# Half of the state's sums behind the scores in two slots of four, products in two halves by tables, and the slots' rows filled from the opening on

## The chip, the cores and the metric

The kernel runs on one core of a Trainium2 chip. The metric is the device time of one execution in microseconds (us), and the median of several executions is what is compared.

## The reference

One transformer block with adaptive layer norm, x of 4 batches by 2048 tokens by 256 features, all in float32:

```
h   = layernorm(x) * (1 + ca) + sa                 # sa, ca, ga, sb, cb, gb from silu(c) @ wmod
q,k,v = h @ w_qkv.T, 16 heads of 16;  q, k = elu(.) + 1
S_t = S_(t-1) + k_t v_t^T ;  z_t = z_(t-1) + k_t   # causal linear attention
o_t = (S_t^T q_t) / max(z_t . q_t, 1e-6)
x   = x + ga * (o @ w_out.T)
h   = layernorm(x) * (1 + cb) + sb
gates: softmax over 8 experts, top 2, capacity 1280 rows for each expert
x   = x + gb * sum over kept experts of gate * (silu(h @ w_gate.T) @ w_down[e].T)
```

## The kernel before

**Stages.** The 8192 tokens are 64 tiles of 128 tokens, and four tiles are a group (16 groups). An opening loads inputs and weights and makes the modulation rows. The attention stage then runs `slot_(it, j, n)` for n = -8 to 73, one tile to a slot (`run_slots`); q = n % 4 says which of the four slots of a group it is. A last stage runs the experts over 40 blocks of 256 gathered rows. Each engine has its own `slot_` in its own order, and the engines meet by semaphores alone.

**A slot on TensorE** (the `slot_` of `block.tensor`), for tile n, in this order: `scores(n)` (32 small products, line 1375; two heads at a time, written to the banks of `SCW`); `from_state(n)` (32 small products, line 1408: what the state from all earlier tiles gives, written to the other half of the same banks, in two rounds `other` = 0 and 1 of 16, the second behind semaphore `scores_run`; its end gives `sc_full`); `columns_and_keys(n)` (lines 1387, 1393); the first projection of the next group (`stage1_qk` m = 0 in q = 1 and m = 2 in q = 2, line 1513; `stage1_v` u = 0 in q = 3, line 1524); in q = 0 `h2_transposes` instead (line 1547), in q = 3 also `positions` (lines 1635 to 1639); `add_to_state(n)` (32 products, line 1458: the state's increment by tile n + 1); `from_tile(n)` (64 products, line 1425: masked scores by values); in q = 0 `stage1_transposes` (line 1498); `out_product(n - 1)` (line 1485); the first `AHEAD` = 2 products of the second projection, `head_rows(n)` (line 1473), and the rest of that projection.

**What the others do for it.** VectorE (`block.vector`) masks the scores behind `sc_full` in two halves (`masked_scores`, line 996, semaphore `sm_done`), multiplies and adds the state (`state`, lines 1027 to 1038, `sbd_done`), divides the heads (`normalise_heads`, line 1012, `an_done`) and adds the out product to x (`add_out`, line 1161). ScalarE evacuates: `AK` (line 802), `h2T` (line 835, `h2t_done`), the values `VA` (line 809, `pj_read`), the heads `OTs` (line 857, `ot_done`), and makes the masked queries `QM` (line 793). GpSimd makes the low half of `hT` (line 569, `h_lo`), the weights `w_og` (line 604), and sends token rows to the experts' slots by indirect DMA (line 519), some of the sends held until `sc_full`, `ak_full` or `av_done`.

**What add_to_state waits for.** In q = 3 the next tile is the first of a new group, so its values come from the projection just before it: it waits for ScalarE's first `VA` of that group. In q = 0 it shares the bank `PM` with the transposes of `h2_transposes`, and waits until ScalarE has copied both halves out (`h2t_done`).

**The fill.** The slots' rows in memory (`xe`, 10,240 rows) get 260 start values each from `erow`, by one DMA that ScalarE issues in `early(11)`, that is after its slot n = 3. Only the first `departure` on GpSimd (slot n = 12) waits for it (`init_out`). `early(j)` runs after slot n = j - 8.

**Numbers.** The projections are fp32r products of a high and a low part (`SPLIT`, three pairs by two chunks: 6 products of 512 columns in `stage1_qk`, 12 of 256 in `stage1_v`). The out product is 2 float32 products of 256 columns, which the profile records as 4.

Of the kernel before, what the change touches and what calls it, by code (L numbers as in the profile page):

```python
# [22 lines left out]
P = 128  # L23
D = 256
# [26 lines left out]
AHEAD = 2  # L51
# [7 lines left out]
def adaln_block(nc, x, wqkv, wo, wr, wg, wd, c, wmod, out, xe, mod_rows):  # L59
    with ExitStack() as ctx:  # L60
# [183 lines left out]
        scores_run = sem("scores_run")  # L244
# [410 lines left out]
        def _(act):  # L655
# [6 lines left out]
            def early(j):  # L662
# [668 lines left out]
        def _(pe):  # L1331
# [31 lines left out]

            def scores(T):
# [13 lines left out]
                last.then_inc(scores_run, 1)  # L1378
# [18 lines left out]
            def from_state(T):  # L1397

                q, gp = T % 4, (T // 4) % 2
                pe.wait_ge(sbd_done, T + 1)  # L1400
                for other in range(2):
                    if other:
                        pe.wait_ge(scores_run, T + 1)
                    for cc in range(DC):
                        for r in range(4):
                            rows, half = slice(32 * r, 32 * r + 32), slice(64 * (r % 2), 64 * (r % 2) + 64)
                            k = (r + other) % 2
                            last = mm(OB[half, k, r // 2, cc, :],  # L1408
                                      Sbd[rows, (2 * T + k) % 4, cc, :, :].rearrange("p s w -> p (s w)"),
                                      QT[rows, gp, cc, q * P + CH * k:q * P + CH * k + CH], start=(cc == 0), stop=False,  # L1410
                                      skip_group_check=True)
                last.then_inc(sc_full, 1)

            def from_tile(T):
# [4 lines left out]
                pe.wait_ge(sm_done, 2 * T + 2)  # L1419
# [56 lines left out]
            def out_product(T):  # L1476
# [7 lines left out]
                for cc in range(DC):  # L1484
                    last = mm(SB[:, 0:D], ATs[:, cc, :], w_ogs[T // TPB % 2][:, cc, :], start=(cc == 0), stop=(cc == DC - 1))  # L1485
# [15 lines left out]
            def stage1_qk(G, m, part=slice(0, 6)):  # L1501
# [6 lines left out]
                elif m >= 2 and part.start == 0:  # L1508
                    pe.wait_ge(pj_read, 6 * N + m - 1)
                for u, ((hp, wp), cc) in list(enumerate(itertools.product(SPLIT, range(DC))))[part]:  # L1510
                    if m == 0 and hp == 1:
                        pe.wait_ge(h_lo, 2 * N + cc + 1)
                    last = mm(PJ[m % 2][:], w_qkv[:, wp, cc, (m + 2) % 4 * P:((m + 2) % 4 + 1) * P], hT[:, hp, cc, :],  # L1513
                              start=(u == 0), stop=(u == 5))
                if part.stop == 6:
                    last.then_inc(pj_full, 1)

            def stage1_v(G, u, part=slice(0, 6)):
                N = G + 1
                if part.start == 0:  # L1520
                    pe.wait_ge(pj_read, 6 * N + 3 + u)
                for t, cc, (i, (hp, wp)) in list(itertools.product(range(2), range(DC), enumerate(SPLIT)))[
                        2 * part.start:2 * part.stop]:
                    last = mm(PJ[u][:, t * D:(t + 1) * D],  # L1524
                              hT[:, hp, cc, (2 * u + t) * P:(2 * u + t + 1) * P],
                              w_qkv[:, wp, cc, 2 * D:3 * D], start=(cc + i == 0),
                              stop=(cc == DC - 1 and i == len(SPLIT) - 1))
                if part.stop == 6:
                    last.then_inc(pj_full, 1)
# [112 lines left out]
            def slot_(it, j, n):  # L1642
# [8 lines left out]
                if tile_ok(n):  # L1651
# [162 lines left out]
```

## Time and profile before

| what | value |
|---|---|
| median of 3 executions | 837.57 us (836.6 to 841.67) |
| the profiled execution | 840.02 us, its span 838.2 us |
| TensorE busy | 760.4 us, 91% of the span |
| VectorE, ScalarE, GpSimd busy | 553.8, 485.7, 489.0 us |
| mean granted TensorE clock | 0.963 |

The page gives busy times by engine, the span in 40 slices, the DMA queues, the chain of work that ended last, and the costliest groups of instructions. "Idle before" is the time an engine stood still ahead of an instruction, with what ended it; "issue" there means that the profile shows no releaser.

### The profile page before, as it was taken

How to read it: one execution, taken by the hardware profiler on the slowest of the kernel's cores; microseconds unless marked ns; L12 is line 12 of the kernel's file. 1: busy time of each engine (PE TensorE's matmuls, PEld its weight loads, DVE VectorE, ACT ScalarE, POOL GpSimd, SP SyncE). 2: the span in 40 equal slices, each digit the busy share in tenths (PEclk: the TensorE clock that was granted, in tenths of full speed). 3: DMA queues.
4: the chain of work that ended last, by engine and by line, in shares of the span. 5: the costliest groups of instructions: out<-in, count | busy, mean ns of one | idle time of the engine just before them, and what ended most of it. 6: DMA issues, size and time to landing. Idle time of an engine off the chain costs nothing.

```text
span 838.2 us, 35024 instructions
## 1 busy us (share of the span) xinstructions
PE 760.4 (91%) x14631; PEld 673.3 (80%) x14631; DVE 553.8 (66%) x1869; ACT 485.7 (58%) x941; POOL 489.0 (58%) x621
## 2 busy tenths in 40 slices
PE   6798799999999999999999998688999998999994
PEld 4676677877777787788777886588999998999993
DVE  6466367778878877777787686524776646766762
ACT  4565466676677677667667665315555453554541
POOL 2202325766666776676685674563665756765765
PEclk9899889999999999999999998869999998999998
DMA  7509822241334142231121121115667655676653
GB/s 251 204 4 334 254 79 71 87 155 66 117 130 142 67 154 79 89 122 68 46 73 61 55 67 42 40 27 182 122 139 167 126 134 138 121 168 144 126 85 44
DMA packets 66861, 96.03 MB, mean 115 GB/s; under 512 B 7683, under 2 KB 48643, under 8 KB 66585
## 3 DMA queue, kind: packets, MB, share of 16 engines
q1 hardware_dynamic: 34136, 50.26, 19.3%
q0 software_dynamic: 21760, 31.66, 16.8%
q10 hardware_dynamic: 10816, 11.96, 4.6%
q8 instruction: 113, 1.85, 1.0%
q14 instruction: 36, 0.29, 0.1%
HBM read 38.97 MB, written 63.36 MB: 122 GB/s over the span
## 4 chain that ended last, share of the span: by engine, by line
PE 78%; issue 7%; POOL 5%; DMA 4%; DVE 2%; ACT 2%; POOLq 0%; ACTq 0%; DVEq 0%; SPq 0%
PE SCW L1746 11%; PE SB L1485 8%; PE SCW L1425 6%; PE SCW L1761 6%; PE PJ L1513 6%; PE PM L1513 5%; PE SCW L1375 5%; PE SCW L1408 4%; PE PM L1473 3%; PE PJ L1524 3%; PE PM L1524 3%; PE PM L1761 3%; PE SB L1761 3%; PE PM L1458 3%; PE PM L1387 2%
## 5 line engine op out<-in xcount | busy, mean ns | idle before, releaser
L519 POOL DMA_INDIRECT slot_rows<-Hrow,sloti x128 | 135.1, 1056 | 59.7 <-issue 27.4
L637 POOL DMA_INDIRECT out<-EX,desti x80 | 126.1, 1577 | 23.8 <-POOL idle L465 11.2
L996 DVE TENSOR_TENSOR Sm<-SCW,tri 128x512 f32<-128x512 f32 x128 | 82.4, 686 | 42.0 <-PE SCW L1408 39.9
L465 POOL TENSOR_TENSOR idle<-mhalf 128x1 f32<-128x1 f32 x136 | 59.5, 437 | 77.7 <-DVE EX L1306 47.9
L569 POOL TENSOR_TENSOR hT<-Sm,hT 128x512 fp32r<-128x512 f32 x30 | 38.3, 1278 | 66.9 <-ACT hT L691 66.1
L706 ACT ACTIVATE N<-X,nb,rs 128x256 f32<-128x256 f32 x128 | 66.2, 589 | 8.2 <-POOL nb L579 4.2
L897 ACT ACTIVATE VA<-SCW 128x512 f32<-128x512 f32 x80 | 47.9, 599 | 39.3 <-PE SCW L1746 38.6
L1425 PE MATMUL SCW<-Sm,VA 64*17 64x64 f32 x4096 | 63.9, 224 | 4.0 <-issue 2.8
L1761 PE MATMUL SCW<-w_qkv,QS 128*128 128x256 f32 x416 | 62.7, 287 | 4.4 <-DVE QS L1278 4.4
L1513 PE MATMUL PM<-hT,w_qkv 128*128 128x512 f32 x192 | 63.6, 441 | 0.0
L857 ACT ACTIVATE OTs<-SCW 128x512 f32<-128x512 f32 x64 | 38.2, 597 | 42.2 <-PE SCW L1425 41.5
L1746 PE MATMUL SCW<-KS,w_g 128*128 128x256 f32 x480 | 62.0, 285 | 0.1
L1746 PE MATMUL SCW<-VS,w_g 128*128 128x256 f32 x480 | 61.9, 285 | 0.0
L802 ACT ACTIVATE AK<-PM 128x512 f32<-128x512 f32 (+1 forms) x66 | 38.7, 586 | 40.0 <-PE PM L1393 39.9
L1161 DVE TENSOR_TENSOR X<-X,SB 128x256 f32<-128x256 f32 x64 | 26.7, 418 | 52.7 <-PE SB L1485 50.7
L1761 PEld LDWEIGHTS SCW<-w_qkv,QS 128*128 128x128 f32 x416 | 57.2, 194 | 4.6 <-issue 4.6
L577 POOL TENSOR_TENSOR rs<-vp,mhalf 128x4 f32<-128x4 f32 x31 | 32.5, 1047 | 47.9 <-DVE vp L1054 47.5
L1425 PEld LDWEIGHTS SCW<-Sm,VA 64*17 64x17 f32 x4096 | 51.9, 93 | 9.2 <-issue 5.8
L1746 PEld LDWEIGHTS SCW<-KS,w_g 128*128 128x128 f32 x480 | 58.3, 189 | 0.3 <-DVE KS L1270 0.3
L1746 PEld LDWEIGHTS SCW<-VS,w_g 128*128 128x128 f32 x480 | 58.3, 189 | 0.0
L793 ACT ACTIVATE QM<-QT,parity 128x256 f32<-128x256 f32 x128 | 57.6, 503 | 0.5 <-DVE QT L1045 0.5
L1513 PE MATMUL PJ<-hT,w_qkv 128*128 128x512 f32 x192 | 54.6, 421 | 0.0
(253 smaller groups left out, 1999.3 us busy)
## 6 DMA issues: line engine op xcount, KB each, us to landing
Hrow<-slot_rows SPq DMA_DIRECT2D x32, 516.0 KB, 3.9
slot_rows<-erow ACTq DMA_DIRECT2D x1, 10400.0 KB, 41.2
X<-x SPq DMA_DIRECT2D x16, 512.0 KB, 5.6
out<-X SPq DMA_DIRECT2D x16, 512.0 KB, 3.6
QT<-slot_rows SPq DMA_DIRECT2D x8, 516.0 KB, 3.8
Hrow<-MB SPq DMA_DIRECT2D x8, 512.0 KB, 3.5
MB<-mod_rows SPq DMA_DIRECT2D x1, 2048.0 KB
slot_rows<-Hrow,sloti POOLq DMA_INDIRECT x128
```

What stands on the lines that cost most here:

```text
L465: pool.tensor_tensor(idle[:, k:k + 1], mhalf[:, 0:1], mhalf[:, 0:1], ALU.add).then_inc(breath, 1)
L519: pool.indirect_dma_start(xe, bass.IndirectOffsetOnAxis(sloti[:, par, k, t:t + 1], 0), Hrow[:, par, t, :], None, bounds_check=last_slot, o ...
L637: pool.indirect_dma_start(out, bass.IndirectOffsetOnAxis(desti[s % 2][:, a:a + 1], 0), Ys[s % 2][:, a, :], None, bounds_check=TOK - 1, oob ...
L706: act.activation(dst, X[:, xt, :], ACT.Identity, scale=rs[:, t:t + 1], bias=nb[:, t:t + 1]).then_inc(s_ready, 1)
L793: act.activation(QM[:, (n + 1) % 2, odd], QT[:, g1 % 2, :, q1 * P:(q1 + 1) * P], ACT.Copy, scale=parity[:, odd:odd + 1]).then_inc(q_masked, 1)
L996: dve.tensor_tensor(Smh(T % 2)[:, 2 * b:2 * b + 2], SCW[:, 2 * b:2 * b + 2, 0:2 * P].rearrange("p r (m i) -> p r m i", i=CH), tri64[:].uns ...
L1425: last = mm(OB[32 * a:32 * a + SW, k, b, cc, :], VA[part(k), gp, q, head(cc, r, s), :], Smh(T % 2)[part(k), r, 2 * cc + s, :], start=False ...
L1485: last = mm(SB[:, 0:D], ATs[:, cc, :], w_ogs[T // TPB % 2][:, cc, :], start=(cc == 0), stop=(cc == DC - 1))
L1513: last = mm(PJ[m % 2][:], w_qkv[:, wp, cc, (m + 2) % 4 * P:((m + 2) % 4 + 1) * P], hT[:, hp, cc, :], start=(u == 0), stop=(u == 5))
L1524: last = mm(PJ[u][:, t * D:(t + 1) * D], hT[:, hp, cc, (2 * u + t) * P:(2 * u + t + 1) * P], w_qkv[:, wp, cc, 2 * D:3 * D], start=(cc + i ...
L1746: last = mm(SC[hh][:, (f % 2) * BW:(f % 2 + 1) * BW], w_g[:, wp, cc, f * P:(f + 1) * P], XT[par][:, xp, cc, :], start=(cc + i == 0), stop= ...
L1761: last = mm(((MA, KR), (MD, SB))[par][a][:, 0:D], hid[par][hp][:, f, a * P:(a + 1) * P], WD[k][wp][:, f, :], start=(f + i == 0), stop=(f = ...
```

## The change

`from_state` now takes the rounds it is to run. In slots with q = 1 or 2 (`APART`, n > 0) round 0 stands directly behind the scores, and round 1 further down, directly ahead of `add_to_state`; in slots with q = 0 or 3 both rounds stand there. `sc_full` is given behind the scores or behind round 0. Semaphore `scores_run` is gone; a call that holds round 1 waits for both halves of the mask (`sm_done`), and `from_tile` behind it no longer does. `AHEAD` is gone: `head_rows` stands ahead of the whole second projection. The products of `stage1_qk` are issued in two column halves where a bit of `HALVED` says so, and the out products where a bit of `PARTED` does. The DMA of the fill moves from `early(11)` to `early(4)`.

```diff
-AHEAD = 2
+HALVED = (12, 14, 12, 10, 0, 8, 10, 2, 8, 10, 0, 12, 10, 0, 8, 10)
+PARTED = (15, 0, 15, 9, 3, 7, 9, 3, 15, 9, 2, 15, 9, 3, 7, 0)
+APART = (1, 2)
...
-                if j == 11:
+                if j == 4:
                     act.wait_ge(consts, N_CONST)
                     act.dma_start(xe[:, 0:D + 4].rearrange("(p n) r -> p n r", p=P),
...
+            def from_state(T, others):
+
+                q, gp = T % 4, (T // 4) % 2
+                for other in others:
+                    if other == others[0]:
+                        pe.wait_ge(sbd_done, T + 1)
+                        if others[-1]:
+                            pe.wait_ge(sm_done, 2 * T + 2)
+                    for cc in range(DC):
...
-                last.then_inc(scores_run, 1)
+                if T > 0 and q in APART:
+                    last = from_state(T, (0,))
+                last.then_inc(sc_full, 1)
...
-                pe.wait_ge(sm_done, 2 * T + 2)
...
+                pieces = 2 if PARTED[T // GT] >> T % GT & 1 else 1
+                for columns in (slice(D // pieces * u, D // pieces * (u + 1)) for u in range(pieces)):
+                    for cc in range(DC):
+                        last = mm(SB[:, columns], ATs[:, cc, :], w_ogs[T // TPB % 2][:, cc, columns],
+                                  start=(cc == 0), stop=(cc == DC - 1))
...
+                pieces = 2 if HALVED[N] >> m & 1 else 1
+                for columns in (slice(GW // pieces * u, GW // pieces * (u + 1)) for u in range(pieces)):
+                    for i, (hp, wp) in enumerate(SPLIT):
+                        for cc in range(DC):
+                            if m == 0 and hp == 1:
+                                pe.wait_ge(h_lo, 2 * N + cc + 1)
...
-                if tile_ok(n):
-                    if n > 0:
-                        scores(n)
-                    from_state(n)
+                if tile_ok(n) and n > 0:
+                    scores(n)
...
+                if tile_ok(n):
+                    from_state(n, (1,) if n > 0 and q in APART else (0, 1))
                 if n >= -1 and tile_ok(n + 1):
                     add_to_state(n, g, routed, step)
...
-                    second_projection(slice(0, AHEAD))
                 if tile_ok(n):
                     head_rows(n)
+                if stage1 and q > 0 and n >= -1:
+                    pe.wait_ge(state_read, n + 2)
                 if stage1:
-                    second_projection(slice(AHEAD, 6))
+                    if q == 1:
+                        if group_ok(gn - 2):
+                            pe.wait_ge(taken, G - 2 + 1)
+                        stage1_qk(G, 1)
+                    elif q == 2:
+                        stage1_qk(G, 3)
+                    elif q == 3:
+                        stage1_v(G, 1)
```

## Rows read from the trace of the kernel before

**Rows 1.** The page: span and busy times by engine.

```profile
span 838.2 us, 35024 instructions
PE 760.4 (91%) x14631; PEld 673.3 (80%) x14631; DVE 553.8 (66%) x1869; ACT 485.7 (58%) x941; POOL 489.0 (58%) x621
```

**Rows 2.** Chain that ended last, slots n = 11 (q = 3), 12 (q = 0): start, us, what.

```profile
126.43 0.62 PE SCW L1375 x32
127.06 0.59 PE SCW L1408 x31
...
128.23 1.41 PE PJ L1524 x12
...
137.20 0.61 ACT h2T L835
```

**Rows 3.** TensorE in order of time: add_to_state, q = 3 and 0, first, last of 13 each.

```profile
130.38 0.36 PE L1458 MATMUL PM<-VA,AK 64*32 64x34 f32 x32 [0.60 <-issue]
137.94 0.36 PE L1458 MATMUL PM<-VA,AK 64*32 64x34 f32 x32 [0.88 <-ACT h2T L835]
...
498.82 0.36 PE L1458 MATMUL PM<-VA,AK 64*32 64x34 f32 x32 [0.60 <-issue]
...
506.38 0.36 PE L1458 MATMUL PM<-VA,AK 64*32 64x34 f32 x32 [0.88 <-ACT h2T L835]
```

**Rows 4.** ScalarE in order of time, slot n = 11.

```profile
129.68 0.60 ACT L809 ACTIVATE VA<-PJ 128x512 f32<-128x512 f32 x1 [0.81 <-PE PJ L1524]
131.50 0.60 ACT L857 ACTIVATE OTs<-SCW 128x512 f32<-128x512 f32 x1 [1.22 <-PE SCW L1425]
```

**Rows 5.** VectorE in order of time: masks of n = 11 and 13, and before the latter.

```profile
127.71 1.29 DVE L996 TENSOR_TENSOR Sm<-SCW,tri 128x512 f32<-128x512 f32 x2 [0.93 <-PE SCW L1408]
...
143.32 0.42 DVE L1165 BATCH_NORM_STATS2 st<-X 128x6 f32<-128x256 f32 x1
143.72 1.29 DVE L996 TENSOR_TENSOR Sm<-SCW,tri 128x512 f32<-128x512 f32 x2
```

**Rows 6.** Chain that ended last, slot n = 10 (q = 2) and out products of n = 9, 12.

```profile
110.23 0.86 PE SB L1485 x4
...
121.10 1.40 PE PJ L1513 x6
...
123.53 1.06 PE SB L1485 x4
...
125.05 0.44 PE PM L1473 x4
```

**Rows 7.** TensorE in order of time, during the fill.

```profile
68.25 0.69 PE L1375 MATMUL SCW<-QM,KT 32*64 32x128 f32 x32
...
71.79 0.27 PE L1387 MATMUL PM<-ident,An 128*128 128x128 f32 x1 [2.00 <-issue]
...
85.59 0.61 PE L1425 MATMUL SCW<-Sm,VA 64*17 64x64 f32 x38 [2.75 <-issue]
...
101.54 0.58 PE L1375 MATMUL SCW<-QM,KT 32*64 32x128 f32 x23 [2.21 <-issue]
...
111.46 0.69 PE L1375 MATMUL SCW<-QM,KT 32*64 32x128 f32 x32
```

**Rows 8.** TensorE in order of time, opening and next group.

```profile
38.33 0.48 PE L1408 MATMUL SCW<-QT,Sbd 32*64 32x64 f32 x7 [1.95 <-issue]
...
142.38 0.69 PE L1375 MATMUL SCW<-QM,KT 32*64 32x128 f32 x32
```

**Rows 9.** The page, DMA queues and the fill's issue: KB, us to landing.

```profile
q8 instruction: 113, 1.85, 1.0%
...
slot_rows<-erow ACTq DMA_DIRECT2D x1, 10400.0 KB, 41.2
```

**Rows 10.** Windows of 20 us: TensorE, its loads, VectorE, ScalarE, GpSimd, clock, DMA share, GB/s.

```profile
20.00:40.00 20.00, 15.55 (x315) 12.98 (x314) 10.25 (x29) 12.17 (x25) 4.98 (x5) 0.87 0.61 213
...
80.00:100.00 20.00, 15.72 (x331) 12.76 (x323) 9.54 (x29) 9.63 (x19) 7.50 (x15) 0.91 1.08 331
```

More of the change, by code:

```diff
@@ L9 @@
-import itertools
 from contextlib import ExitStack
@@ L1362, in early @@
                     pe.wait_ge(w_in, 48)
+            def from_state(T, others):
[6 more added lines that the diff above has]
+                    for cc in range(DC):
+                        for r in range(4):
+                            rows, half = slice(32 * r, 32 * r + 32), slice(64 * (r % 2), 64 * (r % 2) + 64)
+                            k = (r + other) % 2
+                            last = mm(OB[half, k, r // 2, cc, :],
+                                      Sbd[rows, (2 * T + k) % 4, cc, :, :].rearrange("p s w -> p (s w)"),
+                                      QT[rows, gp, cc, q * P + CH * k:q * P + CH * k + CH], start=(cc == 0), stop=False,
+                                      skip_group_check=True)
+                return last
             def scores(T):
@@ L1395, in columns_and_keys @@
                 last.then_inc(ak_full, 1)
[L1397 to L1412, printed above, removed]
             def from_tile(T):
@@ L1507, in stage1_qk @@
                     pe.wait_ge(h_hi, 2 * N + 2)
-                elif m >= 2 and part.start == 0:
+                elif m >= 2:
                     pe.wait_ge(pj_read, 6 * N + m - 1)
[L1510 to L1514, printed above, removed]
@@ L1515, in stage1_qk @@
-                if part.stop == 6:
-                    last.then_inc(pj_full, 1)
-            def stage1_v(G, u, part=slice(0, 6)):
-                N = G + 1
[L1520 to L1529, printed above, removed]
+                pieces = 2 if HALVED[N] >> m & 1 else 1
@@ new lines, in stage1_qk @@
+                for columns in (slice(GW // pieces * u, GW // pieces * (u + 1)) for u in range(pieces)):
[3 more added lines that the diff above has]
+                                pe.wait_ge(h_lo, 2 * N + cc + 1)
+                            last = mm(PJ[m % 2][:, columns], w_qkv[:, wp, cc, (m + 2) % 4 * P:((m + 2) % 4 + 1) * P],
+                                      hT[:, hp, cc, columns],
+                                      start=(cc + i == 0), stop=(cc == DC - 1 and i == len(SPLIT) - 1))
@@ new lines, in stage1_qk, with stage1_v @@
+                last.then_inc(pj_full, 1)
+            def stage1_v(G, u):
+                N = G + 1
+                pe.wait_ge(pj_read, 6 * N + 3 + u)
+                for t in range(2):
+                    for cc in range(DC):
+                        for i, (hp, wp) in enumerate(SPLIT):
+                            last = mm(PJ[u][:, t * D:(t + 1) * D],
+                                      hT[:, hp, cc, (2 * u + t) * P:(2 * u + t + 1) * P],
+                                      w_qkv[:, wp, cc, 2 * D:3 * D], start=(cc + i == 0),
+                                      stop=(cc == DC - 1 and i == len(SPLIT) - 1))
+                last.then_inc(pj_full, 1)
```

17 lines of the change are left out of this document (1 added, 16 removed).

## The prediction

> **What bounds the kernel now.** I read the page first: TensorE is busy for 91% of the span [rows 1]. A share that high says little about where time can be won, so I went on to the chain of waits, which in the attention stage runs from one TensorE piece to the next [rows 2]. The reader is to see there that scores, state products, transposes and projection follow each other without a hole, and that in q = 0 the chain leaves TensorE for ScalarE's copies of h2T, with almost nothing of TensorE in between. Then I looked at TensorE in order of time for every idle stretch. In the steady part there are two in each group. In q = 3 it stands 0.60 us before `add_to_state`, 13 times from tile 11 to tile 59; in q = 0 it stands 0.88 us before it, 13 times from tile 12 to tile 60 [rows 3]. Slots with q = 1 and 2 have none that recurs. The third thing is in the opening third of the attention stage. While the fill's 10.4 MB run (41.2 us from issue to landing [rows 9]), TensorE stands three times for 2 us and more, in the middle of a run of like products or between two alike transposes, with no releaser [rows 7].
>
> **The state's sums, q = 3.** Scores end at 127.06, the 32 state products take 0.59 us, and 0.58 us of transposes lie between them and the values' projection (128.23, for 1.41 us) [rows 2]. ScalarE's VA starts at 129.68 and is over at 130.28, and `add_to_state` starts at 130.38 [rows 3, 4]. So everything up to the projection's end moves 0.59 us ahead, and the 0.59 us of state products fall between that end and the release. The wait is 0.60 us wide, so it holds them: 0.59 us gained. For this the mask must be over when TensorE gets there. The mask takes 1.29 us and starts 0.06 us behind the last state product (127.71 against 127.65) [rows 2, 5]; given behind the scores it runs from 127.12 to 128.41. TensorE arrives at 127.06 + 0.58 + 1.41, at 129.05 or later: 0.6 us spare. Queued behind this wait are the state products, `add_to_state` and `from_tile`, and for these wait VectorE's state and ScalarE's OTs.
>
> **q = 0.** The wait is for the second h2T copy (137.20, for 0.61 us) [rows 2], itself behind transposes that also move 0.59 us ahead. 0.88 us hold 0.59 us, and 0.29 us of wait stay [rows 3]. Gain 0.59 us again.
>
> **How often.** 13 slots of either kind are in the pattern. Tiles 3, 7, 4 and 8 have waits of like width before `add_to_state` in the chain, two for VA, one for AK, one for h2T; I count them at the same worth though they have no rows here. 30 x 0.59 = 17.7 us. If only the q = 3 slots pay, it is 15 x 0.59 = 8.9 us, and that end stays for the range. What is late next: in q = 3 the VA copy still, by 0.01 us; in q = 0 the h2T copy still. In both a further gain would have to come from ScalarE.
>
> **q = 1 and 2.** Half of the products (0.3 us) stay behind the scores, half go ahead of `add_to_state`. There is no hole here for them, so TensorE's sum is as it was: 0. The mask gets its go 0.3 us ahead. In q = 1 VectorE is busy with bn_stats from 143.32 to 143.74 and starts the mask at 143.72 whether the go comes then or at 143.4 [rows 5]; it ends at 145.0, and TensorE needs it after scores, half the sums, the transposes and a projection, about 0.5 us later. The cost of cutting a run of small products in two has no row of its own. The switch from small to full products shows as 0.2 us in the out product (1.06 behind `from_tile`, 0.86 behind transposes [rows 6]), but the number of such switches stays the same; I take 0, with 32 x 0.15 = 4.8 us as the upper end and nothing below, as nothing shortens.
>
> **head_rows ahead of the projection.** It now comes 0.47 us sooner behind the out product. It waits for OTs: started 0.04 us behind `from_tile` (131.50) and 0.60 us long [rows 4], against an out product of 1.06 us [rows 6]. 0.4 us spare, so 0. If that cover went (ScalarE late by more than 0.4 us in a slot), each late 0.1 us would be 0.1 us of TensorE. VectorE gets the heads 0.47 us sooner, which helps the masks.
>
> **Halves.** The tables hold 23 set bits for projections and 37 for out products. 6 products of 512 columns take 1.40 us [rows 6], 12 of 256 take 1.41 us with as many weight loads [rows 2]: 23 x 0.01 = 0.2 us at most, I take 0. An out product of 256 columns is recorded as 4 in 0.86 us; halved it is 8 of 128 columns, and transposes of that width go at 4 in 0.44 us [rows 6], so 0.88. 37 x 0.02 = 0.7 us; I take 1.1 us, since its weight loads are not those of a transpose. Ends: 0.94 us by the pace of the 12 halves, 37 x 0.08 = 3.0 us; and 37 x -0.20 = -7.4 us if a shorter first product hid the switch. I am near the first, as a weight load has to wait for the small products whatever follows it.
>
> **The fill.** From the scores of tile 5 (68.25) to those of tile 9 (111.46) it is 43.2 us; from there to tile 13 (142.38) 30.9 us [rows 7, 8]. So the fill costs 12.3 us where it lies: 7.0 us of standing (2.00 + 2.75 + 2.21) and 5.3 us of half clock behind it (granted 0.91 between 80 and 100 us, with a DMA share of 1.08 [rows 10]). The stalls have the look of instructions that come late: instructions are loaded by DMA too, 113 pieces with 1.85 MB [rows 9]. Issued in `early(4)` the fill starts near 15 us. ScalarE has nothing due there for some microseconds, so the issue itself is free. But it now meets the modulation rows and the x tiles of the opening, where the DMAs are 0.61 busy between 20 and 40 us [rows 10]. Some 15 MB (10.4 of the fill, 2 of modulation rows spread to all partitions, 0.5 for each group of x) at 331 GB/s [rows 10] take 45 us and end past 60 us, over the slots of tiles 0 to 4. One stall of this kind is there already, 1.95 us at tile 1 [rows 8]. TensorE issues about as many products as in the old place, so I expect three stalls again where one is: two more at 12.3 / 3 = 4.1 us. Gain 12.3 - 8.2 = 4.1 us. Ends: 12.3 us if the opening hides all, and -4.1 us if there are five stalls in it (four more, 16.4 us).
> The Trainium skill's page "Runtime: NRT & Kernel Launch", section "Instruction fetch mechanics", says that instructions come in lines of 16 KiB, prefetched in sequence, and that this is hidden because they are dispatched more slowly than they are fetched. The size agrees with the trace (1.85 MB in 113 pieces are 16.4 KB each); that it is hidden does not, by the 2 us stalls of [rows 7]. By that page the fill would cost nothing in either place, and the sum would be 4.1 us higher; that is the third rival below.
>
> **The end.** In the last tile VectorE is the late one, and the sums now lie behind its mask: +0.6 us, my estimate from the 0.59.
>
> **The sum.** -17.7 - 4.1 + 1.1 + 0.6 = -20.1 us. Against the profiled execution, 840.0, that gives 819.9. That execution is 2.4 us above the median of the three, so the forecast is **817.5 us**.
>
> **Rivals.** (1) The opening hides the fill altogether: 12.3 instead of 4.1, 809.3 us. For it: few TensorE instructions before 27 us. Against: the stall at 38 us [rows 8] with no fill at all. (2) Only one of the two waits is filled, because the release moves along with the sums: 8.9 us less, 826.3 us. For it: q = 0 hangs on three copies in a row on ScalarE. Against: ScalarE idles ahead of them. (3) Moving the fill is worth nothing, be it that it never cost anything or that it costs as much in the opening: 821.6 us. (4) The other side: the masks. All of q = 1 to 3 now wait for `sm_done` ahead of the sums, 0.3 to 0.6 us sooner than `from_tile` did. It decides if VectorE ends the mask over 0.5 us later than I put it, that is, if one more of its large steps (1.29 us [rows 5]) comes ahead. Then 1.29 - 0.5 = 0.8 us in each of 48 slots, 38 us: 817.5 + 38 = 856 us. For it: VectorE runs straight into the mask in q = 1 [rows 5]. Against: in q = 3 it idles 0.93 us before it. (5) The fill starves the opening in each of five slots: 817.5 + 8.2 = 825.7 us.
>
> **How the numbers follow.** The forecast 0.50, (1) 0.12, (2) 0.12, (3) 0.13, (4) 0.04, (5) 0.09. The range takes in (1) almost, (2) and (5): 809 to 829 us. About 1% is what a measurement of this kernel can tell from no change, so faster means below 829.2. Chances: faster 0.88 (all but (4) and some of the tails of (2) and (5)), same 0.08, slower 0.04.
>
> **What would show it.** In the profile after: no idle time, or 0.1 us, before `add_to_state` or the sums in q = 3, and about 0.3 us in q = 0; a steady group 1.2 us shorter, near 29.7 us, where it is 30.9 (tile 9 to tile 13, [rows 7, 8]); no idle time with VectorE's mask as releaser before the sums; the DMAs busy from 15 to past 60 us and nearly free from 70 to 105, and tiles 5 to 9 in about 30 us; one to three more stalls of 2 us before 65 us. It is wrong if groups keep their length (the waits moved along), if the sums wait for the mask, or if tiles 0 to 5 grow by as much as tiles 5 to 9 shrink.

## The result: slower by 1.3%, and the profile after

The changed kernel takes 849.26 us (median of 4, 843.07 to 855.42) where the one before takes 839.62 (836.6 to 843.54) beside it: ratio 1.0133, 95% interval 1.0085 to 1.0181. The forecast was 817.5 us, its range 809 to 829, with a chance of 0.04 for slower. The profiled execution took 847.79 us, 7.8 more than the one before. The times here and below are medians of all executions, while the ratios leave out executions over 1.5% above the fastest of the same kernel, so that a ratio need not be the quotient of its two medians.

The page of the kernel after: span, busy times, granted clock and DMA by slice, the instruction queue and the fill (packets, MB, share; then KB and us to landing).

```profile
span 846.1 us, 35628 instructions
PE 770.0 (91%) x14917; PEld 687.1 (81%) x14917; DVE 548.0 (65%) x1869; ACT 484.6 (57%) x941; POOL 490.0 (58%) x621
...
PEclk9989999999999999999999999869999999999997
DMA  9992023142244131232021121114676666677553
...
q8 instruction: 115, 1.88, 1.0%
...
slot_rows<-erow ACTq DMA_DIRECT2D x1, 10400.0 KB, 49.5
```

TensorE is busy for 9.6 us more, the fill takes 49.5 us to land instead of 41.2 [rows 9], and the DMAs are full from the start, as intended. The idle time of TensorE, by what ended it (us in total, times, longest):

```profile
PE SB L1489 <- issue: 13.7, 7, 4.8
...
PE PM L1460 <- issue: 5.1, 2, 3.4
PE SCW L1427 <- issue: 4.6, 4, 1.3
...
PE SCW L1376 <- issue: 2.5, 3, 1.8
PE SCW L1376 <- DVE Sm L996: 2.2, 3, 1.0
...
PE PM L1407 <- DVE An L1012: 1.9, 4, 1.1
```

And of the kernel before, the same view's first two lines:

```profile
PE PM L1458 <- ACT h2T L835: 12.2, 14, 0.9
PE PM L1458 <- issue: 11.1, 16, 1.8
```

Of the 30 waits ahead of `add_to_state` (L1460 after), 23 us, three short ones are left, 0.8 us together, and two long ones that are something else: the wait of 1.8 us at tile 0, and a stall of 3.4 us that belongs to what follows. What has come is idle time marked "issue" in the middle of out products (L1489) and of `from_tile` (L1427), where nothing that the profile shows holds TensorE. The wait for the mask, which was my rival on the other side, is there three times, for 2.2 us in all.

The sums do go into the waits. TensorE in order of time, in a slot with q = 3 (`add_to_state` stood 0.60 us before, [rows 3]):

```profile
157.74 0.69 PE L1376 MATMUL SCW<-QT,Sbd 32*64 32x64 f32 x32
...
158.41 0.36 PE L1460 MATMUL PM<-VA,AK 64*32 64x34 f32 x32
```

And this is what takes it back, from 119 us on (start, us, what ran; in brackets the idle time ahead of it):

```profile
118.97 0.36 PE L1460 MATMUL PM<-VA,AK 64*32 64x34 f32 x32
119.21 0.86 PE L1427 MATMUL SCW<-Sm,VA 64*17 64x64 f32 x64
122.10 1.05 PE L1489 MATMUL SB<-w_og,AK 128*128 128x128 f32 x8 [2.03 <-issue]
...
214.17 0.94 PE L1489 MATMUL SB<-Sm,AK 128*128 128x128 f32 x6 [1.71 <-issue]
229.86 0.62 PE L1427 MATMUL SCW<-Sm,VA 64*17 64x64 f32 x24 [1.16 <-issue]
...
285.63 0.52 PE L1427 MATMUL SCW<-Sm,VA 64*17 64x64 f32 x34 [1.29 <-issue]
...
312.60 1.66 PE L1489 MATMUL SB<-w_og,AK 128*128 128x128 f32 x7 [2.29 <-issue]
...
406.74 1.29 PE L1489 MATMUL SB<-w_og,AK 128*128 128x128 f32 x7 [1.55 <-issue]
```

Behind the stall of 2.29 us TensorE also runs on a lower clock. The window 310 to 315 us (length, then busy us and instructions of PE, PEld, DVE, ACT, POOL, granted clock, DMA share, GB/s):

```profile
310.00:315.00 5.00, 2.71 (x14) 2.63 (x14) 1.65 (x6) 1.39 (x3) 4.13 (x7) 0.68 0.27 103
```

The same stages of both executions, worked out from TensorE's rows in order of time (from the start of `scores` of one tile named to that of the other; a group is the slots q = 0 to 3; us):

```
                            before   after
tile 0 to tile 4             34.61   44.51
tile 4 to tile 9             49.80   36.07
tile 9 to tile 61           398.49  408.68
from tile 61 to the end     328.25  329.87
fastest group of 4 slots     30.46   29.56
```

So the fill moved (+9.9 and -13.7, 3.8 us gained), the best group is 0.9 us shorter, and yet 13 groups together are 10.2 us longer. Slot by slot, q = 3 went from 7.95 to 7.37 us and q = 0 from 8.04 to 7.50, where no stall falls in them. Over those 13 groups TensorE's idle time fell only from 21.5 to 19.0 us, though some 18 us of waits were filled, and its busy time grew from 377.0 to 389.7 us.

### The profile page after: what moved, and what is told of

Read it like the earlier page. It is cut to its first block, busy times and chain, and to the rows that moved or that the text cites. A ratio compares the mean times of both kernels' runs of the same rounds, so it can differ in the third digit from the quotient of the medians.

```text
span 846.1 us, 35628 instructions
## 1 busy us (share of the span) xinstructions
PE 770.0 (91%) x14917; PEld 687.1 (81%) x14917; DVE 548.0 (65%) x1869; ACT 484.6 (57%) x941; POOL 490.0 (58%) x621
## 4 chain that ended last, share of the span: by engine, by line
PE 75%; issue 8%; POOL 5%; DVE 5%; DMA 4%; ACT 1%; POOLq 0%; DVEq 0%; ACTq 0%; SPq 0%
PE SCW L1748 9%; PE SB L1489 8%; PE SCW L1427 6%; PE PM L1521 6%; PE PJ L1521 5%; PE SCW L1763 5%; PE SCW L1376 4%; PE SCW L1393 4%; PE PM L1475 3%; DMA out<-EX,desti 3%; PE PJ L1532 3%; PE PM L1407 3%; PE PM L1460 2%; PE PM L1532 2%; PE PM L1763 2%
## 5 line engine op out<-in xcount | busy, mean ns | idle before, releaser
L519 POOL DMA_INDIRECT slot_rows<-Hrow,sloti x128 | 139.0, 1086 | 67.6 <-issue 27.0
L1427 PE MATMUL SCW<-Sm,VA 64*17 64x64 f32 x4096 | 63.4, 222 | 4.8 <-issue 4.6
L1427 PEld LDWEIGHTS SCW<-Sm,VA 64*17 64x17 f32 x4096 | 52.4, 92 | 9.8 <-issue 7.9
L1376 PEld LDWEIGHTS SCW<-QT,Sbd 32*64 32x64 f32 x2048 | 42.9, 133 | 20.5 <-issue 19.4
L1376 PE MATMUL SCW<-QT,Sbd 32*64 32x64 f32 x2048 | 52.8, 225 | 5.1 <-issue 2.5
L1521 PE MATMUL PM<-hT,w_qkv 128*128 128x256 f32 (+1 forms) x306 | 55.4, 326 | 0.3
## 6 DMA issues: line engine op xcount, KB each, us to landing
slot_rows<-erow ACTq DMA_DIRECT2D x1, 10400.0 KB, 49.5
```

Of the source, the lines that this page charges most:

```text
L519: pool.indirect_dma_start(xe, bass.IndirectOffsetOnAxis(sloti[:, par, k, t:t + 1], 0), Hrow[:, par, t, :], None, bounds_check=last_slot, o ...
L1376: last = mm(OB[half, k, r // 2, cc, :], Sbd[rows, (2 * T + k) % 4, cc, :, :].rearrange("p s w -> p (s w)"), QT[rows, gp, cc, q * P + CH * ...
L1427: last = mm(OB[32 * a:32 * a + SW, k, b, cc, :], VA[part(k), gp, q, head(cc, r, s), :], Smh(T % 2)[part(k), r, 2 * cc + s, :], start=False ...
L1521: last = mm(PJ[m % 2][:, columns], w_qkv[:, wp, cc, (m + 2) % 4 * P:((m + 2) % 4 + 1) * P], hT[:, hp, cc, columns], start=(cc + i == 0), s ...
```

## What the stalls have in common

I counted TensorE's instructions in the trace (each weight load and each product is one, semaphore instructions too; a float32 product that is recorded twice counts twice) up to every idle stretch over 1 us between 26 and 505 us, and took the count modulo 256:

```
before        26.7 (1.81) 147; 38.3 (1.95) 194; 71.8 (2.00) 193; 85.6 (2.75) 193; 101.5 (2.21) 194
after         26.7 (1.78) 171; 34.0 (3.36) 193; 40.3 (1.75) 194; 48.8 (4.76) 194; 63.1 (1.64) 194;
              68.2 (1.06) 194; 122.1 (2.03) 193; 214.2 (1.71) 194; 229.9 (1.16) 193; 285.6 (1.29) 194;
              312.6 (2.29) 193; 329.6 (1.15) 194; 406.7 (1.55) 194
before_shift  28.9 (1.80) 19; 37.1 (1.79) 194; 74.1 (2.07) 194; 81.0 (1.36) 193; 94.6 (2.34) 194;
              101.8 (2.10) 194
shift         29.9 (1.79) 19; 37.9 (2.56) 194; 70.8 (2.93) 194; 77.8 (1.55) 193; 91.8 (2.40) 194;
              100.8 (3.59) 194; 112.1 (1.21) 194; 143.3 (1.27) 194; 228.9 (2.89) 194; 270.6 (1.08) 193;
              327.2 (1.11) 230; 384.4 (1.77) 193; 455.7 (1.26) 194
```

(Start in us, length, count modulo 256; the last two kernels are experiments below, with 128 instructions more ahead of tile 0, which shows in the first count: 147 + 128 is 19 modulo 256.) The first stall of each is the wait at tile 0. All the others but one stand at 193 or 194; that one, 327.2 in `shift`, ends by the profile with VectorE's division of the heads. The instruction queue moves pieces of 16,384 bytes [rows 9]; 256 instructions to a piece make 64 bytes each. I call 256 instructions from one such place to the next a line. The packets of that queue have start times, and set against the crossings they give (counted from the trace; "lasts" includes the stall at its end):

```
         crossed at   next fetch starts    line lasts   stall at its end
before      64.81           +4.72             7.00          2.00
before      78.93           +4.40             6.66          2.75
before      93.25           +5.72             8.29          2.21
before     112.29           +2.31             4.69          0.26
after       40.31           +5.78             8.50          4.76
after      116.33           +3.36             5.77          2.03
after      208.38           +2.98             5.79          1.71
after      280.39           +2.82             5.24          1.29
after      306.28           +3.42             6.33          2.29
after      132.63           +0.41             3.62          0
after      157.91           +0.35             3.17          0.08
after      181.21           +0.63             4.17          0
```

There is one packet to a line. When a line is crossed, the packet for the line after it mostly starts within 1.5 us: between 112 and 505 us in 58 of the 79 lines of the kernel before and in 50 of 78 after. In 14 and 21 lines it starts 1.5 to 2.4 us behind the crossing, in 3 and 7 later than that (at most 3.6 us), and in 4 lines of the kernel before up to 0.9 us ahead of it. While the fill runs it is 3 to 6 us in most lines. In the rows with a stall TensorE goes on 2.3 to 2.9 us behind the packet's start; most packets take 0.9 to 1.4 us, with the fill or without. So TensorE stands when it uses up a line sooner than the lag and these 2.3 to 2.9 us allow. The 20 traces of this case bear this out without an exception: between 26 and 505 us they hold 1,814 lines, none is entered less than 2.18 us behind the start of its own packet, and all 149 stalls of 1 us or more at a line end are over 2.2 to 3.2 us behind it.

Without stalls, between 112 and 505 us, the kernel before has 9 of 79 lines under 4 us (shortest 3.59) and the one after 24 of 78 (shortest 2.94), because its state sums now stand beside `add_to_state` and `from_tile`: 128 small products, 256 instructions, in 1.7 us. In the row of 40.31, the longest stall of all, the lag of 5.78 us does most of it: it would have stopped any line under 8 us.

That line ends are where it happens is tested below by moving them; what makes a fetch late is not found.

## The experiments

The kernels ran on five chips, in the groups below. On two of these chips the kernel before takes 870 us, on the others 838 to 840, so each is compared with the kernel before on its own chip. Stages and stalls are those of the one profiled execution, and the executions of one kernel differ by 0.5 to 3%: those of `sums_only`, `no_tables`, `broken_run` and `q03_only` were the slowest of their kernels, those of `pieces` and `q03_shift` the fastest.

**The parts alone: the sums.** `sums_only` is the kernel before with the sums placed as after, old product order otherwise:

```diff
                if tile_ok(n) and n > 0:
                    scores(n)
...
+                if tile_ok(n):
+                    from_state(n, (1,) if n > 0 and q in APART else (0, 1))
```

> Theory L (instruction lines): TensorE stands where its 256-instruction lines end, if the next line was asked for late or the present one is used up in under about 4 us. Moving the sums gains 0.9 us a group (29.56 where it was 30.47), and the lines cross elsewhere: 840 - 13 = 827 us, give or take 6 for the stalls, all of them at one remainder modulo 256. Rival O (order): the new order itself is what stalls, because 128 small products in one run use up a line in 1.7 us wherever it starts: stalls of 15 us or more after tile 9, and at least 840 us.

846.01 us, ratio 1.0046 (0.9999 to 1.0094) to 839.95; by the medians 1.0072. It is the rival that came, not the 827 us. Its fastest group is 29.46 us, 1.0 under the kernel before, and still tile 9 to tile 61 takes 408.46 us (398.49 before). Its stalls at line ends behind tile 9 are 18, with 16.3 us (before: 4, with 1.4). Its idle time by what ended it, over the whole span:

```profile
PE SCW L1427 <- issue: 9.3, 9, 1.7
...
PE SB L1487 <- issue: 6.1, 4, 2.3
PE SCW L1393 <- issue: 6.1, 4, 2.4
```

The gain and the stalls are both in this part of the change. The comparison of times alone hardly tells it from the kernel before; the groups and the stalls in the trace do.

**The fill alone.**

```diff
-                if j == 11:
+                if j == 4:
```

> Theory L: the fill delays the fetches of lines by 3 to 5 us wherever it lies. Tiles 4 to 9 lose their 12 us, tiles 0 to 4 get about 10 us longer: -2 us, 838 us. Rival F: the move of the fill by itself is the loss (+5 us or more, 845 us). What I forecast first (-4.1 us) would be 835.5 us.

837.37 us, 0.9962 (0.9918 to 1.0006). Tiles 0 to 4 are 5.5 us longer, tiles 4 to 9 are 12.0 shorter: 6.4 us on balance in that execution, some 3 by the medians.

**The halves alone.**

```diff
+                pieces = 2 if PARTED[T // GT] >> T % GT & 1 else 1
+                for columns in (slice(D // pieces * u, D // pieces * (u + 1)) for u in range(pieces)):
```

> Theory L: halves cost nothing by themselves and only shift the lines in an order with few dense runs: stalls change by a few us either way, 836 to 845 us. Rival H: the halved products are slow in themselves (over 0.1 us each for 60 of them): 846 us or more, in every halved product and not at line ends.

845.39 us, 1.0067 (1.0026 to 1.0107), and the profiled one took 848.56. By itself a halved projection takes 1.67 us against 1.645, a halved out product 1.158 against 1.131 (medians of the rows): 23 x 0.03 + 37 x 0.03 = 1.8 us. The rest: stalls at line ends, 2.5 us more before tile 9 and 2.2 more behind it, since 286 more products with their loads move every line end; and the experts' stage, 333.1 us against 328.3. That stage lies between 326 and 338 us over all kernels here with nothing changed in it, so I don't read its 4.9 us as an effect.

**The change without its tables.**

```diff
-HALVED = (12, 14, 12, 10, 0, 8, 10, 2, 8, 10, 0, 12, 10, 0, 8, 10)
-PARTED = (15, 0, 15, 9, 3, 7, 9, 3, 15, 9, 2, 15, 9, 3, 7, 0)
+HALVED = (0,) * 16
+PARTED = (0,) * 16
```

> The changed kernel with both tables at zero. Theory L: the lines cross elsewhere, so the stalls move to other tiles and their sum after tile 9, 15.5 us in the changed kernel, becomes another number (4 to 20 us): 830 to 848 us, with the clean groups still at 29.5 us. Rival O: 15 us of stalls stay, 848 us. Rival H: the halves were the loss, 10 us less, 838 us, and no stalls at line ends.

840.63 us (831.45 to 858.09), 0.9957 (0.9907 to 1.0007). The profiled execution was the slowest, 858.09, with 17 stalls of 19.4 us behind tile 9 and 16.1 us at half the clock. By the medians it is 1.0008, no change. The tables, which compute nothing of their own, make some 9 us of difference by the medians (849.26 against 840.63, not side by side; less the 1.8 us that the halved products take); what a table does to the length of a program is part of what it costs.

**Is it the line end, or the burst?** Three kernels on the base of `sums_only`, and one for the fill, all against 837.46 us. `shift` puts 32 tiny float32 products ahead of the opening's `modulation(0)`. The trace has them as 64 products and 64 weight loads, 128 instructions, so all lines end half a line earlier in the program:

```diff
                 if j == 4:
+                    for _ in range(32):
+                        mm(SB[0:BATCH, 0:BATCH], cS[:, 0, :], cS[:, 0, :], start=True, stop=True, skip_group_check=True)
```

> As sums_only, but 32 tiny products (128 instructions) are added in the opening, where TensorE waits for a DMA, so that every line end later on falls half a line away. Theory L: each stall goes to another place, remainder again one value modulo 256 (194 + 0, since the lines themselves are fixed, while the products in them shift by 128); their sum after tile 9 may be 5 to 20 us instead of 16, and the median may move by up to 8 us either way. Rival (stalls belong to places in the slot, such as the masks or copies): the same tiles stall as in sums_only, sum and median unchanged within 2 us.

854.82 us, 1.0204 (1.0111 to 1.0298). The stalls are at 193 and 194 again (table above), so at other places of the program: that they belong to line ends is shown by this. Which lines hit is luck: 11 stalls with 11.2 us behind tile 9 instead of 18 with 16.3, but 14.4 us instead of 9.5 ahead of it, where the fill runs. Its opening is also 2 to 3 us later.

`spaced` holds back SyncE's loads and stores of a group until single tiles are done, so that they don't come at once:

```diff
+                sp.wait_ge(x1_done, min(g * GT + GT + 1, TILES))
...
+                sp.wait_ge(x1_done, min(g * GT + GT + 2, TILES))
```

> As sums_only, but the three transfers of 0.5 MB that leave and enter at the end of a group are issued one tile apart instead of in one burst. Theory L, in the form that the other half of a stall is a fetch that starts 2.5 to 4 us late behind such a burst: late fetches (over 2.4 us) get rare after tile 9, stalls there fall from 16 us to about 9, median about 840 us. Rival: the line length alone decides, stalls stay near 16 us and the median at 846.

843.56 us, 1.0075 (1.0027 to 1.0123), again the rival: 20 stalls of 15.6 us, and fetches that start over 2.4 us late 8 times (6 in `sums_only`). The late fetches don't come from these transfers standing together.

`broken_run` puts the out product between `add_to_state` and `from_tile`, so that 128 small products no longer stand together:

```diff
-AHEAD = 2
+AHEAD = 3
...
                     add_to_state(n, g, routed, step)
+                if tile_ok(n - 1):
+                    out_product(n - 1)
```

> As sums_only (sums moved, nothing else), but the out product stands between add_to_state and from_tile, so that the run of 128 small products is cut by 0.9 us of long ones; three products of the second projection cover OTs instead of two. Theory L, in the form that a line used up in under 4 us is the danger: the shortest lines get 0.9 us longer, lines under 4 us go from 23 to about 10 as before the change, stalls after tile 9 from 16 us to under 8, and the median from 846 to about 838 us. Rival O2 (the sums' place itself, whatever lies between): stalls stay at 16 us and 846 us.

855.07 us, 1.0208 (1.013 to 1.0287). Lines under 4 us fell from 23 to 10 and the stalls from 16.3 to 10.2 us, with 13 fetches over 2.4 us late where `sums_only` has 6. But the fastest group is 31.5 us, 2 us more, and the expected 838 us did not come. A slot with q = 2 takes 0.24 us more (7.41 for 7.17) with no idle time, which I put to the switch to large products in mid-run and back; in q = 0 and 1 TensorE also waits for ScalarE's copies of `VA` and `hT`, 8.3 us between 112 and 505 us. It bears out the length of lines and is of no use.

`pieces` sends the fill as 8 DMAs of 1.3 MB behind slots n = 0 to 7, from the kernel before:

```diff
-                if j == 11:
+                if j >= 8:
                     act.wait_ge(consts, N_CONST)
-                    act.dma_start(xe[:, 0:D + 4].rearrange("(p n) r -> p n r", p=P),
-                                  erow[:].to_broadcast([P, SLOTS // P, D + 4])).then_inc(init_out, 16)
+                    act.dma_start(xe[:, 0:D + 4].rearrange("(p n) r -> p n r", p=P)[:, 10 * (j - 8):10 * (j - 7), :],
+                                  erow[:].to_broadcast([P, 10, D + 4])).then_inc(init_out, 16)
```

> The kernel before, with the fill cut in 8 DMAs of 1.3 MB, one in each slot from tile 0 to tile 7. Theory L: what stalls TensorE in the fill is that a fetch starts 4 to 6 us after it is asked for; behind 1.3 MB (4 us of queue) it starts at most 4 us late and often on time. Stalls in the fill from 9.4 to about 4 us, 840 to about 834 us. Rival (the fill's bytes cost what they cost): 840 us.

834.17 us, 0.9982 (0.9943 to 1.0021), by the medians 0.9961. Tiles 4 to 9 take 41.6 us (49.8), tiles 0 to 4 are as they were: 8.2 us less in that execution, which the comparison doesn't bear out as a gain.

**Other orders of the sums,** against 870.35 us. `out_first` leaves `from_state` in place and fills the two waits with the previous tile's out product:

```diff
+                first = stage1 and q in (0, 3) and tile_ok(n - 1)
+                if first:
+                    out_product(n - 1)
                 if n >= -1 and tile_ok(n + 1):
```

> The kernel before with its sums where they were; instead the out product of the tile before goes ahead of add_to_state in q = 0 and q = 3 (0.86 us, 8 instructions, no small products), to fill the same two waits with long work. In q = 3 three products cover OTs. Theory L: the run of small products stays at 96 and lines under 4 us stay near 9, so stalls after tile 9 stay under 5 us, and the waits are filled without giving the time back: 0.86 us in q = 0, about 0.3 us in q = 3 (there it waits for VectorE's reading of the positions): 15 x 1.2 = 18 us, from 838 to about 821 us. Rival W: any filling of the two waits brings the lines nearer to each other and so the stalls: stalls of 10 us or more, 832 us or more.

876.65 us, 1.0053 (1.0012 to 1.0094), where 2% less was expected. The q = 0 slot falls from 8.84 to 8.0 us and the q = 1 slot behind it grows from 7.95 to 8.8: a filled wait that comes back in the next slot. In q = 3 TensorE now waits for VectorE's positions instead, 12 times, 6.1 us in all, and the slot stays at 8.0 us. With the fill in pieces on top:

> out_first with the fill in 8 pieces from tile 0 to tile 7. If the two are independent: out_first less 3 us, about 818 us. If shorter lines meet the pieces: no better than out_first.

870.48 us, 0.9999 (0.9968 to 1.0029).

`q03_only` moves the sums in the slots with the waits (q = 0 and 3) and leaves q = 1 and 2 wholly as they were:

```diff
+                if q not in APART:
+                    last.then_inc(sc_full, 1)
+                    return
+                last.then_inc(scores_run, 1)
+                from_state(T, (0, 1)).then_inc(sc_full, 1)
```

> The sums moved in slots q = 0 and q = 3 alone; in q = 1 and 2 both rounds stand behind the scores as before. Theory L: the runs of 128 small products are in q = 0 and 3 and these stay; the ones of 112 are gone. Stalls after tile 9 fall from 16 us to about 12, 843 us. Rival A (the split in q = 1 and 2 was the loss, half a run between two full products): stalls under 6 us and 830 us.

858.13 us, 0.9813 (0.973 to 0.9896) from four executions, by the medians 0.9860: the first whose interval lies below 1. 8 stalls with 5.1 us behind tile 9.

`before_shift` puts the 128 instructions of `shift` into the kernel before:

> The kernel before with the same 32 tiny products in the opening as in shift, so that its line ends fall half a line away. Theory L in its stronger form: in the old order no line is used up in under 3.5 us wherever it starts, so stalls after tile 9 stay under 5 us (1.4 us in the kernel before); with 1 to 3 us for the products themselves 838 to 842 us. Rival P (the kernel before only happened to have its line ends at good places, and any shift costs as much as in the moved order): stalls after tile 9 of 10 us or more and 850 us.

871.72 us, 1.0008 (0.9964 to 1.0052), 3 stalls with 1.5 us, 2 lines under 4 us. Where lines are long, as here, where they end made no difference that can be told. Its granted clock was at half for 17.1 us between 112 and 505 us all the same.

**Does it hold?** Against 871.48 us, on another chip: `q03_only` again, with the fill in pieces, with the 128 instructions, and the change itself.

> The same kernel as q03_only, beside the changed kernel. Theory Q (most of the line stalls come with the split sums in q = 1 and 2): stalls after tile 9 near 5 us as on the other chip, and 2 to 12 us below the kernel before. Rival (q03_only was fast only because that chip is slow in another place): stalls of 12 us or more, and above the kernel before.

> q03_only with the fill in 8 pieces. If pieces give what they gave alone (3 us), 3 us below q03_again, the fastest so far.

> The changed kernel itself, on the chip of this call. Its loss holds if it is 5 to 14 us above the kernel before, with 10 to 20 us of stalls after tile 9 at line ends; the loss was one chip's or one load's if it is below the kernel before.

> q03_only with the 32 tiny products in the opening, line ends half a line away. Theory A (the place of the line ends decides): stalls after tile 9 move to other tiles and their sum may double or halve against q03_again, up to 10 us in the median. If q03's few stalls are a matter of structure, they stay within 3 us of q03_again, and the median within 3 us plus 2 for the tiny products.

862.21 us (four executions, 0.9894 by the medians, no interval; 9 stalls, 5.6 us); with pieces 861.36, 0.9881 (0.9844 to 0.9919); the change 865.79, 0.9937 (0.9905 to 0.9968); with 128 instructions 870.8, 0.9993 (0.996 to 1.0025), where the stalls before tile 9 are 16.6 us instead of 11.0. So on this chip the change itself is faster than the kernel before, by 0.6%. By what was said ahead of that run its loss belongs to one kind of chip, and on that kind the change as a whole has the four executions of the result alone. And 128 idle instructions take away the gain of `q03_only`. In the two traces (864.81 and 860.28 us, 4.5 us of the 8.6 between the medians) it is all in the opening and the fill: tile 9 is reached 6.6 us later, 2.4 of them ahead of tile 0, where the added products run; from there to tile 61 the shifted kernel is 1.3 us shorter.

**On a chip where the kernel before takes 839.6:**

> q03_only again, to see it on a chip where the kernel before takes 840 us. If the call lands on such a chip: the waits of q = 0 and 3 filled (-0.9 us a group, 13 groups, 12 us), stalls after tile 9 near 5 us where sums_only had 16, half clock under 7 us: about 833 us, 0.5 to 1% below the kernel before. If the alternation of small and long products costs as much as in sums_only: 846 us. On a chip at 870 us it repeats its 1 to 2% gain.

> q03_only with the fill in 8 pieces, on the same chip: 3 us below q03_third if the pieces add what they gave alone on the chip at 837 us, the same if they do not.

836.0, 0.9897 (0.9846 to 0.9947), and with pieces 833.27, 0.9879 (0.9802 to 0.9956). By the medians it is 0.9957 and 0.9925, so the gain on this chip is 0.4 to 1%, and 0.8 to 1.2% with pieces. Groups take 29.34 us at best. It still has 10 stalls at line ends behind tile 9, 8.6 us. One of them in the chain that ended last:

```profile
125.01 0.62 PE SCW L1379 x32
125.63 0.34 PE PM L1465 x23
125.97 0.71 PE SCW L1432 x59
126.68 1.31 issue
127.98 0.21 PE SCW L1432
```

The version with pieces lies under the kernel before on either kind of chip, by 1.2% where that takes 871 us, and under the change itself there (861.36 to 865.79). What the pieces add to `q03_only` is not told from nothing by these runs: 0.9 us on one chip and 2.7 on the other, with four executions on one side of each comparison.

```
                     9 to 61   fastest   stalls at line ends, us     lines < 4 us   half clock
                        us     group     to tile 9    behind it      behind tile 9  112-505 us
before                398.49    30.46       9.4       1.4 (4)             9            0
after                 408.68    29.56      12.9      15.1 (15)           24           10.2
sums_only             408.46    29.46       9.5      16.3 (18)           23           10.2
fill_only             402.04    30.09       8.1       4.8 (6)             9            0
halves_only           401.34    30.51      11.9       3.5 (7)            11            0
no_tables             415.21    29.47       7.6      19.4 (17)           20           16.1
shift                 404.94    29.31      14.4      11.2 (11)           21           13.7
pieces                399.55    30.45       7.2       2.5 (4)             9            0
q03_third             398.69    29.34      11.1       8.6 (10)           24            6.8
q03_pieces_again      395.88    29.36      12.1       8.1 (11)           25            3.4
on the chips at 870 us
before_shift          428.86    32.68      11.0       1.5 (3)             2           17.1
q03_only              419.92    31.56      11.1       5.1 (8)            11           10.2
after_again           426.06    31.48      11.8       9.2 (11)           10           10.2
```

("Behind it" ends with tile 61.) Short lines and late fetches have to meet. Fetches over 2.4 us late between 112 and 505 us: `halves_only` has 8 of them and 11 short lines and stands for 3.5 us; `sums_only` has 6 with 23 short lines and stands for 16.3 us. The changed kernel has 7, `q03_third` only 4 with as many short lines, and they stand for 15.1 and 8.6 us; the kernel before has 3, `before_shift` 4, both with few short lines. So the count of short lines says that a kernel is open to these stalls, not how many it will have. On the chips at 870 us, where the slots are longer by themselves, the change has 10 short lines instead of 24.

## Why the prediction was wrong

**The state's sums, q = 3: right.** The wait of 0.60 us held the 0.59 us of products: the slot went from 7.95 to 7.37 us. **q = 0: right in size,** 8.04 to 7.50, 0.54 where I had 0.59. The 0.29 us of wait that I left there did not stay, though: from the first sum to `add_to_state` it is 0.79 us (165.18 to 165.97) where I had 0.59.

**How often: this is the step that failed,** "30 x 0.59 = 17.7 us". Slots without a stall did give their 0.54 to 0.6 us, but behind tile 9 these are 10 of 13 with q = 3 and 5 of 13 with q = 0. I priced the move as if 32 products put beside others cost nothing beyond their own time. They made 128 small products in a row, and TensorE's instructions then ran out at line ends: 15.1 us of stalls behind tile 9 against 1.4. I had noted under the fill that stalls of 2 us "have the look of instructions that come late", and charged them to the fill's 10 MB alone. None of my rivals had this one.

For tile 9 to tile 61, +10.2 us: 13 groups x -0.9 = -11.8; stalls +13.7; about 10 us of it at half the granted clock, which is worth some 5 by the 1.2 GHz against 2.4; the halves that fall in these tiles +1.4; 1.9 left over. The 5 and the 1.9 are my accounting, not a measurement.

**q = 1 and 2: near my upper end.** I took 0, with 4.8 us as the end. q = 2 is as it was (7.26 to 7.22); q = 1 grew from 7.22 to 7.50, which is 0.28 us in each of 16 slots, 4.5 us (0.23 of it is there in `sums_only` too). The runs of `q03_only`, which leave these slots alone, have the better ratio on both kinds of chip, though only on the one at 871 us did the change itself run beside them; they don't part the split in itself from the shorter lines that go with it.

**head_rows:** no loss of its own is to be seen; the waits for the heads' copies stayed away. **Halves:** 1.8 us for 1.1 in products, and with the program's length moved, 1.0067 as a whole. That is some 5.5 us by the medians where the sum had 1.1, and none of my ends for it had a price for the length.

**The fill: right in size.** "Gain 12.3 - 8.2 = 4.1 us": measured 3.8 in the changed kernel, 6.4 alone, some 3 by medians. The way was as put: four stalls over 1.5 us in the opening where one was, the longest 4.76 us. (The 5.3 us that I put to half clock are more than the cited row gives, 0.09 of 20 us; the window 68.25:111.46 has a granted clock of 0.84, which bears them out.) "Runtime: NRT & Kernel Launch" of the Trainium skill, section "Instruction fetch mechanics", calls the fetch of lines mostly hidden. The trace agrees on their size, and on 256 instructions to one; hidden it is only while a line lasts longer than the fetch's lag and the 2.3 to 2.9 us behind it, as the 15 stalls behind tile 9 show, with no fill running.

**The masks:** three waits, 2.2 us in all. My 0.5 us of spare time held nearly everywhere. The 0.04 that I gave to slower was for the masks; slower came, and by another way.

**The signs I had named:** no idle time before `add_to_state` in q = 3 (right; in q = 0 about 0.3 us were to stay, and next to nothing did), group near 29.7 us (right at best, 29.56; on the mean of 12 groups 31.3 where before has 30.7, and this is where the sign failed), tiles 5 to 9 in 30 us (right: 29.8 from scores to scores, where it was 43.2), DMAs full from the start and nearly free from 70 us (right). Every sign I would have looked at in one slot was there, and the kernel was slower.

## What to carry to other kernels

Before moving small products together, count TensorE's instructions (load and product are two) and see how long each 256 of them last: under some 4 us, the time for them isn't always theirs alone. Idle time inside a run of like products, with no releaser, is to be set against that count before it is put down to anything else. And a gain worked out from single slots must be held against a longer stretch with all of its stalls; a change of a program's length by 128 instructions went with 1% in `q03_shift`, and with nothing in `before_shift`.

## What I had not expected of the hardware

Line ends: TensorE never goes on sooner than 2.18 us behind the start of the packet of 16,384 bytes that it needs, in 1,814 lines. That start comes within 1.5 us of the crossing before it in most quiet lines, and after 3 to 6 us in most while a 10.4 MB transfer runs. Why some are late with no large transfer about stays open: spacing the loads and stores changed nothing.

At some stalls the granted clock falls to 0.5, 1.2 GHz, for several us (0.68 on the mean of 310 to 315 us): in the changed kernel at the stalls that end at 229.9, 312.6 and 406.7 us, and not at those of 122.1 and 214.2, which are as long. `fill_only` has none of it behind 112 us, while `before_shift` has 17.1 us with hardly a stall at a line end. So half clock isn't the stalls' doing alone, and the 5 us above are no more than an account.

Two kinds of chip: where the kernel before takes 870 us, slots with q = 1 and 2 take 7.95 us instead of 7.22, by a pause of 0.35 to 0.7 us inside `from_tile` or ahead of it, not at line ends. From `before_shift`:

```profile
186.71 0.43 PE L1427 MATMUL SCW<-Sm,VA 64*17 64x64 f32 x10
187.62 0.79 PE L1427 MATMUL SCW<-Sm,VA 64*17 64x64 f32 x54 [0.48 <-issue]
```

Ten products ran, then nothing for 0.48 us, then the other 54. What it is stays open. The change gains there what it loses here, and the waits are not the reason: in q = 3 the slot goes from 7.95 to 7.37 us on either chip. What is less there is the stalls behind tile 9, 9.2 us for 15.1, beside the fewer short lines, and the slots with q = 2 get shorter (7.96 to 7.79). That the longer slots are the reason fits the rule of the lines; no run here tests it.
